# The first unit's bias features: spread over the rows by TensorE instead of by a DMA round trip, with the first sampling hats moved among the first tiles

## The chip, the cores and the metric

The kernel runs on one core of one Trainium2 chip. The metric is the device time of one execution in microseconds. Before the change it is 891.61 us, the median of three runs (891.41 to 891.81). All engines named here belong to that one core: TensorE (PE, with its weight loads PEld), VectorE (DVE), ScalarE (ACT), GpSimd (POOL) and SyncE (SP), which only issues DMAs.

## The reference

Two layers of the same block run over an image batch of 2 x 128 x 32 x 32. The part that matters is the attention with a learned position bias. Each of 8 groups (16 channels each) gets 64 keys, whose places come from a small convolution (offsets) and where the image is sampled bilinearly. Every one of the 1024 queries sees every key through a bias made by a small network on the signed logarithm of their distance:

```python
off = tanh(einsum('bchw,oc->bohw', gelu(conv(qg, off_dw_w) + off_dw_b), off_pw_w)) * OFF_SCALE
kv = grid_sample(xn, vgrid_scaled)                       # bilinear, 64 keys for each group
pos = grid_q[:, :, None, :] - grid_kv[:, None, :, :]     # 1024 queries x 64 keys x (x, y)
bias = sign(pos) * log1p(abs(pos))
bias = relu(bias @ cpb_w1 + cpb_b1)                      # 2 -> 32
bias = relu(bias @ cpb_w2 + cpb_b2)                      # 32 -> 32
bias = (bias @ cpb_w3 + cpb_b3)                          # 32 -> 1
attn = softmax(qh @ kh * scale + bias)
x = x + out_w @ (attn @ v) + out_b;  x = x + mlp(bn2(x))
```

## The kernel before

The work is cut into 4 segments (layer x image), each into 4 units (pairs of groups, 128 keys on 128 partitions after packing), each unit into 16 steps (2 halves of the queries x 8 strides of keys). So there are 256 steps. One step `g` is: DVE's `first_layer(g)` writes one buffer `h1` (128 x 2048) as the maximum of an x-term and a y-term; PE's `corrections` put a bf16 correction into two PSUM pairs; PE's `layer2(g)` multiplies `h1` by the second layer's weights in 16 tiles of 32 x 32; ACT's `relu2` empties the pairs; PE's `layer3` adds into the scores. There are three `h1` buffers, so DVE may be three steps ahead of PE.

The x- and y-terms (`hxy`) need, for each unit, the features of 128 keys laid over rows in another way than they were computed: key on the free axis, hidden unit on the partitions, each value repeated over 32 partitions. Before the change all 16 units get that layout by DMA: SP stores `feat` to DRAM (`store_features`), loads it back broadcast (`load_features`), and DVE's `hidden_terms` scales it in place.

Nothing is scheduled by a planner. Each engine runs a list of its own: first the list `PROLOGUE` in its order, then step by step its part of the step and behind it the stages that a table puts at that step (`LATE_SLOTS` for what the first segment still owes, `BEFORE_SLOTS` and `AFTER_SLOTS` for later segments). Engines meet only through semaphores. Eight banks of PSUM serve as three pairs handed out in the order in which PE fills them (`ring()`, `turn`, `filled`, `emptied`) and two score banks.

The first segment's own preparation stands in the prologue: normalised image, queries, convolution, offsets, positions, then two branches. One leads to the features and to the first `h1`. The other leads to the sampling weights: PE's `spread` lays the 64 x 2 key coordinates over all partitions, ACT's `spread_out` and eight `distances` take absolute distances, DVE's `hats` turn them into hat functions (`hat_x`, `hat_y`, the latter in `big`), DVE's `hat_products` multiply them into eight `bilinear` pieces, and PE's `sample` uses them. On DVE the prologue ends with `hats`, `hats`, `hidden_terms`. `hat_products` stand behind step 2, `sample` at step 3. PE's `keep_busy` runs four dummy matmuls at the start and four more once the terms are there.

On SP's queue the first segment is stored as features, one part of the `fy` weights (`fy_part`), the load of unit 0, the other `fy` parts, and then `load_fy`, which waits until all six `fy` stores are in DRAM.

Of the kernel before, what the change touches and what calls it, by code (L numbers as in the profile page):

```python
# [10 lines left out]
ALU = mybir.AluOpType  # L11
# [10 lines left out]
HID = 32  # L22
# [10 lines left out]
PAIRS = G // 2  # L33
# [32 lines left out]
for _name, _n in [("ident", 128), ("gridq", W), ("gridkv", 2), ("neg_x", 1), ("neg_y", CHUNKS), ("ones", 32), ("own", 2),  # L66
# [39 lines left out]
LATE_SLOTS = {("dve", "hat_products", 0): 2, ("dve", "hat_products", 1): 2,  # L106
              ("pe", "sample", 0): 3, ("dve", "sample_out", 0): 4, ("pe", "keys_values", 0): 5,
              ("act", "keys_values_out", 0): 5}
# [57 lines left out]
RELEASES = {"up_last": MLP_PARTS, "spread": 2, "keys_values": 5, "attend": 2, "mlp_up": 2}  # L166
RING_STAGES = ("u_rows", "q", "image_t", "offset", "spread", "sample", "keys_values", "scores_t", "attend",
# [35 lines left out]
def build(nc, x_in, consts, weights, x_out, features_dram, fy_dram, reciprocals_dram):  # L203
    with ExitStack() as ctx:
# [44 lines left out]
        h2 = [[sb(f"h2_{j}{k}", [128, ROWS // 2, HALF]) for k in range(H2_BUFS)] for j in range(2)]  # L249
        w1y_of_key = sb("w1y_of_key", [128, 128])  # L250
# [39 lines left out]
        terms_ready = sem("terms_ready")  # L290
        w1y_ready = sem("w1y_ready")
# [70 lines left out]
        def _(sp):  # L362
# [73 lines left out]
            for unit in range(UNITS):  # L436
# [20 lines left out]
        def _(pool):  # L457
# [8 lines left out]
            stages = {"widen_max": widen_max}  # L466
# [3 lines left out]
            for g in range(LAST_STEP + 1):  # L470
                for name, n in PLAN["pool"].get(g, []):
                    stages[name](n)

        @block.scalar
        def _(act):
# [48 lines left out]
            def features(seg):  # L524

                if seg:
# [10 lines left out]
            def spread_out(seg):  # L537
# [4 lines left out]
                emptied("spread", seg, act.activation(key_y, here[:, bank(1)], ACT.Copy))  # L542

# [36 lines left out]
            def gelu_last(part):  # L580
                for c in range(MLP_PARTS):
# [5 lines left out]
                      "offset_tanh": offset_tanh, "features": features, "spread_out": spread_out,  # L587
# [23 lines left out]
        def _(dve):  # L611
# [9 lines left out]
            def first_layer(g):  # L621
# [4 lines left out]
                if g % UNIT_STEPS == 0:  # L626
                    dve.wait_ge(terms_ready, 2 * (unit + 1))
# [125 lines left out]
            def hidden_terms(unit):  # L753
# [3 lines left out]
                dve.wait_ge(feat_loaded[p], 16 * ROWS * (unit // 2 + 1))  # L757
# [82 lines left out]
            for name, n in PLAN["dve"][-1]:  # L840
                stages[name](n)
# [347 lines left out]
```

## Time and profile before

| | |
|---|---|
| median of 3 runs | 891.61 us |
| the profiled execution, its own time | 894.96 us |
| its span, first to last instruction | 893.2 us |
| PE busy | 92% of the span |
| DVE busy | 81% |
| ACT busy | 74% |
| POOL busy | 7% |
| mean granted TensorE clock | 0.983 of full speed |

The profile is one execution. A busy share averages over the whole span, so a question on the start is put to the views of the start: the chain of waits (followed back from the last instruction, from each piece of work to what released it), the timeline (instructions in order of time, equal ones that follow each other merged, with the idle time before them) and the table of stretches (busy time of each engine in each stretch, with the granted TensorE clock). Step 0 of the 256 reaches PE at about 38 us, so everything before is a lead-in that no step overlaps.

### The profile page before, as it was taken

Reading aid. Unit: us, or ns where it says so; the run is one execution under the profiler, and the core shown is the slowest. Engines: PE = TensorE matmul, PEld = TensorE weight load, DVE = VectorE, ACT = ScalarE, POOL = GpSimd, SP = SyncE. Lnnn points to the kernel's source line nnn. Section 1 sums busy time; section 2 is a strip of 40 time slices with the busy share of each in tenths; the row PEclk is TensorE's granted clock in tenths of the full one; section 3 lists DMA queues with packets and bytes.
Section 4 is the critical chain, followed back from the end, with each engine's and each line's share of the span. In section 5 each row is a group of like instructions: output and inputs, shape, how many; then the busy total and the mean of one; then the engine's idle time right before and its main releaser. Section 6 shows DMA issues by size and latency. Waiting matters only on the chain.

```text
span 893.2 us, 27554 instructions
## 1 busy us (share of the span) xinstructions
PE 820.4 (92%) x12486; PEld 235.6 (26%) x12486; DVE 727.8 (81%) x532; ACT 662.1 (74%) x742; POOL 62.5 (7%) x39
## 2 busy tenths in 40 slices
PE   4699998889999999988999999988999999999997
PEld 2222222222222222222222222222222222222224
DVE  5899898898868689799885879979888668989843
ACT  2468778968777688896776877797777668888863
POOL 1000101000010100101010010100101001010110
PEclk8699999999999999999999999999999999999999
DMA  4502020020200102002020200102002020200000
GB/s 167 118 3 49 2 48 3 12 66 2 63 15 17 34 3 49 12 19 49 2 62 15 48 1 14 37 12 57 11 5 60 14 48 3 73 3 3 3 15 24
DMA packets 18264, 27.67 MB, mean 31 GB/s; under 512 B 10980, under 2 KB 11620, under 8 KB 18148
## 3 DMA queue, kind: packets, MB, share of 16 engines
q1 hardware_dynamic: 18148, 25.91, 11.7%
q8 instruction: 99, 1.62, 0.8%
q14 instruction: 17, 0.14, 0.1%
HBM read 23.05 MB, written 2.74 MB: 29 GB/s over the span
## 4 chain that ended last, share of the span: by engine, by line
PE 68%; ACT 14%; DVE 10%; issue 7%; DMA 1%; SPq 0%; ACTq 0%; POOLq 0%
PE pair L887 24%; PE scores L905 22%; ACT h L481 7%; PE pair L861 6%; DVE h L629 5%; PE pair L1040 3%; PE scores L916 3%; PE pair L995 2%; DVE big L742 2%; PE pair L1031 2%; PE pair L1013 2%; PE scores L1001 1%; ACT big L548 1%; ACT big L577 1%; ACT L577 1%
## 5 line engine op out<-in xcount | busy, mean ns | idle before, releaser
L629 DVE TENSOR_TENSOR h<-hxy 128x2048 f32<-128x2048 f32 x256 | 582.6, 2303 | 71.8 <-PE pair L887 67.8
L481 ACT ACTIVATE h<-pair 128x1024 f32<-128x1024 f32 x512 | 518.7, 1025 | 154.3 <-PE pair L861 113.5
L887 PE MATMUL pair<-h,wts 32*32 32x512 f32 x8192 | 300.0, 604 | 20.7 <-DVE h L629 7.7
L905 PE MATMUL scores<-h,wts 128*32 128x512 f32 x2048 | 275.6, 608 | 0.1
L463 POOL CAST neg_max_wide<-neg_max 128x512 fp32r<-128x512 f32 x32 | 59.3, 1853 | 808.0 <-DVE neg_max L765 808.0
L861 PE MATMUL pair<-fy,u_rows 32*128 32x512 bf16 x1024 | 102.6, 387 | 0.0
L887 PEld LDWEIGHTS pair<-h,wts 32*32 32x32 f32 x8192 | 66.0, 103 | 82.1 <-ACT h L481 36.2
L861 PEld LDWEIGHTS pair<-fy,u_rows 32*128 32x128 bf16 x1024 | 26.4, 91 | 217.2 <-issue 217.2
L905 PEld LDWEIGHTS scores<-h,wts 128*32 128x32 f32 x2048 | 42.0, 108 | 156.2 <-issue 147.5
L995 PE MATMUL pair<-const,probs 128*128 128x128 f32 x128 | 20.1, 280 | 21.6 <-ACT h L481 20.8
L491 ACT ACTIVATE probs<-scores,wts 128x512 f32<-128x512 f32 x32 | 22.0, 689 | 23.7 <-PE scores L905 23.5
L765 DVE TENSOR_REDUCE neg_max<-pair 128x8 f32<-128x512 f32 x32 | 22.1, 690 | 21.4 <-PE pair L995 21.2
L916 PE MATMUL scores<-qpad,keys_t 128*32 128x512 f32 x256 | 33.3, 592 | 0.0
L1031 PE MATMUL pair<-work,wts 128*128 128x512 f32 x56 | 27.3, 613 | 0.4
L1040 PE MATMUL pair<-big,wts 128*128 128x512 f32 x56 | 25.9, 605 | 1.1 <-ACT big L577 1.0
L995 PEld LDWEIGHTS pair<-const,probs 128*128 128x128 f32 x128 | 13.4, 140 | 49.8 <-issue 48.1
L794 DVE SCALAR_TENSOR_TENSOR x<-pair,wts,x 128x512 f32<-128x512 f32 x7 | 5.3, 751 | 25.9 <-PE pair L1040 25.9
L569 ACT ACTIVATE probs<-scores,wts 128x512 f32<-128x512 f32 x32 | 21.9, 685 | 4.8 <-PE scores L1001 4.6
L577 ACT ACTIVATE big<-pair,wts 128x512 f32<-128x512 f32 x28 | 17.7, 684 | 8.5 <-PE pair L1031 8.4
L1001 PEld LDWEIGHTS scores<-ident_r,neg_max_wide 128*128 128x128 f32 x128 | 17.2, 190 | 24.4 <-issue 23.0
L1001 PE MATMUL scores<-ident_r,neg_max_wide 128*128 128x128 f32 x128 | 23.0, 302 | 0.6 <-POOL neg_max_wide L463 0.6
L548 ACT ACTIVATE big<-work,const 128x512 f32<-128x512 f32 x32 | 21.0, 721 | 0.0
(106 smaller groups left out, 359.9 us busy)
## 6 DMA issues: line engine op xcount, KB each, us to landing
hxy<-features_dram SPq DMA_DIRECT2D x64, 256.0 KB, 4.8
wts<-weights_dram SPq DMA_DIRECT2D x2, 960.0 KB, 8.3
att_den<-reciprocals_dram SPq DMA_DIRECT2D x7, 256.0 KB
x<-x_dram SPq DMA_DIRECT2D x2, 512.0 KB, 5.7
fy<-fy_dram SPq DMA_DIRECT2D x16, 64.0 KB
fy_dram<-fy_part SPq DMA_DIRECT2D x24, 32.0 KB, 3.9
out_dram<-x SPq DMA_DIRECT2D x3, 256.0 KB, 5.4
features_dram<-pos_sign SPq DMA_DIRECT2D x4, 128.0 KB, 2.5
```

The source lines that it names most:

```text
L463: pool.tensor_copy(neg_max_wide[:], neg_max[phase % 2][:].unsqueeze(2).broadcast_to([128, CHUNKS, NKV]))\
L481: emptied("z", 2 * g + j, act.activation(h2[j][g % H2_BUFS][:].rearrange("p r n -> p (r n)"), pair_of("z", 2 * g + j)[:], ACT.Relu))
L577: emptied("mlp_up", n, act.activation(mlp_h[:, c, bank(half % 2)], pair_of("mlp_up", n)[:, bank(k)], ACT.Gelu, bias=w(half // 2 // B, "mlp ...
L629: dve.tensor_tensor(h1[g % H1_BUFS][:].rearrange("p c (y x) -> p c y x", x=W), hx[unit % 2][:, :, t].unsqueeze(2).broadcast_to([128, CT, H ...
L861: return pe.matmul(z_of(g, r), u_rows[unit // PAIRS // B][key_rows(r)], y.unsqueeze(2).broadcast_to([32, H // 2, W]), **flags)
L887: ins = pe.matmul(z_of(g, r)[32 * c:32 * (c + 1)], w(l, "w2")[key_rows(r), key_rows(r)], h1[g % H1_BUFS][key_rows(r), c], start=r >= 2, st ...
L905: ins = pe.matmul(scores[phase % 2][32 * r:32 * (r + 1)], w(l, "w3")[:, 32 * t:32 * (t + 1)], h2[rows[0] // 2][step % H2_BUFS][:, r % 2], ...
L916: ins = pe.matmul(scores[phase % 2][k], keys_t[seg % 2][:, u, k], qpad[seg % 2][:, 1 + H // 2 * h:1 + H // 2 * (h + 1), 1:W + 1], start=Fa ...
L995: ins = pe.transpose(pair_of("scores_t", phase)[:, s], probs[:, unit % PAIRS, bank(h)][:, s], cst("ident"))
L1001: ins = pe.matmul(scores[phase % 2][:, 128 * k:128 * (k + 1)], neg_max_wide[:, 2 * k:2 * (k + 1)].rearrange("p n j -> p (n j)"), ident_r[: ...
L1031: ins = pe.matmul(pair_of("mlp_up", n)[:, bank(k)], w(half // 2 // B, "mlp_w1")[:, 128 * c:128 * (c + 1)], xn2[:, bank(half % 2)], start=T ...
L1040: ins = pe.matmul(pair_of("mlp_down", half)[:, 0:HALF], w(half // 2 // B, "mlp_w2")[:, 128 * c:128 * (c + 1)], mlp_h[:, c, bank(half % 2)] ...
```

## The change

For unit 0 alone, the DRAM round trip of the features goes. PE's new `first_spread` writes the features straight into two PSUM pairs: 64 matmuls for each pair, each 32 rows by 32 columns with 64 moving columns, whose weight is one column of the identity repeated 32 times, so that it copies one key's features to 32 partitions. The four matmuls that follow each other use the four diagonal 32 x 32 tiles and write four different partition groups of the same PSUM columns. From the first pair ACT makes half of the terms (`first_terms`, two activations with scale and bias), from the second DVE makes the other half (two `tensor_scalar`). ACT needs the negated `w1y`, which DVE computes ahead of `norm1` (`neg_w1y`).

Orders move with it. On PE `u_rows` and four `keep_busy` matmuls stand before `offset`; `first_spread` stands behind `spread`; the second `keep_busy` now waits for DVE's `first_terms`. On DVE `hats` leave the prologue: the first stands behind step 1, the second behind step 2, and DVE's half of `hat_products` behind step 3. The other half of `hat_products` goes to POOL. `sample`, its copy and `keys_values` stand one step later. On SP all six `fy` stores come first, then the store of the features, `load_fy`, and the load of unit 1, which no longer waits for the terms of unit 0.

```diff
 PROLOGUE = {
-    "pe": ["q", "image_t", "offset", "spread", "u_rows"],
-    "act": ["q_out", "image_t_out", "conv_gelu", "offset_tanh", "features", "spread_out"] + ["distances"] * 4,
+    "pe": ["q", "image_t", "u_rows", "keep_busy", "offset", "spread", "first_spread", "first_spread"],
+    "act": ["q_out", "image_t_out", "conv_gelu", "offset_tanh", "features", "spread_out", "first_terms"] + ["distances"] * 4,
     "dve": ["norm1", "w1y_rows", "conv_products", "conv_products", "conv_sum", "conv_sum", "positions", "features_sign",
-            "fy_weights", "hats", "hats", "hidden_terms"],
+            "fy_weights", "first_terms"],
+    "pool": ["hat_products"],
 }
-LATE_SLOTS = {("dve", "hat_products", 0): 2, ("dve", "hat_products", 1): 2,
-              ("pe", "sample", 0): 3, ("dve", "sample_out", 0): 4, ("pe", "keys_values", 0): 5,
...
+LATE_SLOTS = {("dve", "hats", 0): 1, ("dve", "hats", 1): 2, ("dve", "hat_products", 1): 3,
+              ("pe", "sample", 0): 4, ("dve", "sample_out", 0): 5, ("pe", "keys_values", 0): 6,
...
-                if unit == 1:
-                    sp.wait_ge(terms_ready, 2)
...
-            for unit in range(UNITS):
+
+            store_fy(0, (0, 1, 2))
+            store_features(0)
+            load_fy(0)
+            for unit in range(1, UNITS):
...
+            def hat_products(n):
+
+                pool.wait_ge(hats_ready, 1)
+                for k in range(CHUNKS // 2):
+                    pool.tensor_tensor(bilinear[:, k], hat_y[:, k], hat_x[:], ALU.mult).then_inc(bilinear_ready[0], 1)
...
+            def first_terms(n):
+
+                act.wait_ge(first_scale_ready, 1)
+                wait_filled(act, "first_spread", 0)
+                here = pair_of("first_spread", 0)[:].rearrange("p (j a q) -> p a j q", a=2, q=W)
+                for xy, scale_of, bias_of in ((0, w(0, "w1x"), w(0, "b1")), (1, neg_w1y[:], 0.0)):
+                    out = hxy[0][:, xy].rearrange("p c t q -> p (c t) q")[:, 0:CT * STRIDES // 2]
+                    ins = act.activation(out, here[:, xy], ACT.Identity, bias=bias_of, scale=scale_of)
+                    emptied("first_spread", 0, ins)
...
-                if g % UNIT_STEPS == 0:
-                    dve.wait_ge(terms_ready, 2 * (unit + 1))
+                if g == 0:
+                    wait_emptied(dve, "first_spread", 0)
+                    wait_emptied(dve, "first_spread", 1)
+                elif g % UNIT_STEPS == 0:
+                    dve.wait_ge(terms_ready, 2 * unit)
...
+            def first_terms(n):
+
+                wait_filled(dve, "first_spread", 1)
+                here = pair_of("first_spread", 1)[:].rearrange("p (j a q) -> p a j q", a=2, q=W)
+                half = CT * STRIDES // 2
+                out = [hxy[0][:, xy].rearrange("p c t q -> p (c t) q")[:, half:2 * half] for xy in range(2)]
+                emptied("first_spread", 1, dve.tensor_scalar(out[0], here[:, 0], w(0, "w1x"), w(0, "b1"), ALU.mult, ALU.add))
+                emptied("first_spread", 1, dve.tensor_scalar(out[1], here[:, 1], w(0, "w1y"), -1.0, ALU.mult, ALU.mult))
...
+            dve.tensor_scalar(neg_w1y[:], w(0, "w1y"), -1.0, None, ALU.mult).then_inc(first_scale_ready, 1)
...
+            def first_spread(n):
+
+                pe.wait_ge(feat_ready, 1)
+                turn("first_spread", n)
+                half = CT * STRIDES // 2
+                for j in range(half):
+                    for r in range(ROWS):
+                        key = 32 * r + half * n + j
+                        ins = pe.matmul(pair_of("first_spread", n)[key_rows(r), 2 * W * j:2 * W * (j + 1)],
+                                        cst("ident")[key_rows(r), key:key + 1].broadcast_to([32, HID]),
+                                        feat[key_rows(r), 0:2 * PAIRS:PAIRS], start=True, stop=True)
+                filled("first_spread", n, ins)
...
-            pe.wait_ge(terms_ready, 1)
-            keep_busy(4)
+            wait_emptied(pe, "first_spread", 1)
+            keep_busy()
```

PE's order in the lead-in before the change, from the dummy matmuls to the first step (`scores<-keys_t` is `keep_busy`, `pair<-const,coord` is `spread`, `pair<-wts,w1y_of_key` is `u_rows`, `pair<-h_0,wts` is `layer2`):

```order
L1073 MATMUL scores<-keys_t 128x512 x4
L940 MATMUL pair<-work,wts 128x512 x2
L947 MATMUL pair<-const,work 128x128 x8
L955 MATMUL pair<-wts,conv_act 64x8 x2
L964 MATMUL pair<-const,coord 128x128 x8
L934 MATMUL pair<-wts,w1y_of_key 128x128
L1073 MATMUL scores<-keys_t 128x512 x4
L861 MATMUL pair<-fy,u_rows 128x512 x2
L887 MATMUL pair<-h_0,wts 32x512 x16
```

and after it (`pair<-pos_sign,const` is `first_spread`, since `feat` is the tile `pos_sign`):

```order
L1119 MATMUL scores<-keys_t 128x512 x4
L976 MATMUL pair<-work,wts 128x512 x2
L983 MATMUL pair<-const,work 128x128 x8
L970 MATMUL pair<-wts,w1y_of_key 128x128
L1119 MATMUL scores<-keys_t 128x512 x4
L991 MATMUL pair<-wts,conv_act 64x8 x2
L1000 MATMUL pair<-const,coord 128x128 x8
L1012 MATMUL pair<-pos_sign,const 32x64 x128
L1119 MATMUL scores<-keys_t 128x512 x4
L897 MATMUL pair<-fy,u_rows 128x512 x2
```

`u_rows` and one block of dummy matmuls moved ahead of `offset`, and 128 small matmuls stand between `spread` and the last dummy block.

DVE's order around the first steps before the change (`hat_x`, `big` 128x2048 are `hats`, `hxy` is `hidden_terms`, `h_...` one step's first layer, `big<-big,hat_x` the products, `sampled` the copy behind `sample`):

```order
L733 TENSOR_SCALAR hat_x<-hat_x 128x512
L736 TENSOR_SCALAR big<-big 128x2048 x2
L758 TENSOR_SCALAR hxy<-hxy,wts 128x1024
L759 TENSOR_SCALAR hxy<-hxy,wts 128x1024
L826 TENSOR_SCALAR scale<-wts 128x1 x2
L629 TENSOR_TENSOR h_0<-hxy 128x2048
L629 TENSOR_TENSOR h_1<-hxy 128x2048
L629 TENSOR_TENSOR h_2<-hxy 128x2048
L742 TENSOR_TENSOR big<-big,hat_x 128x512 x8
L629 TENSOR_TENSOR h_0<-hxy 128x2048
L629 TENSOR_TENSOR h_1<-hxy 128x2048
L749 TENSOR_TENSOR sampled<-pair,const 128x128
```

and after it:

```order
L793 TENSOR_SCALAR hxy<-pair,wts 128x512
L794 TENSOR_SCALAR hxy<-pair,wts 128x512
L861 TENSOR_SCALAR scale<-wts 128x1 x2
L655 TENSOR_TENSOR h_0<-hxy 128x2048
L655 TENSOR_TENSOR h_1<-hxy 128x2048
L759 TENSOR_SCALAR hat_x<-hat_x 128x512
L762 TENSOR_SCALAR big<-big 128x2048
L655 TENSOR_TENSOR h_2<-hxy 128x2048
L762 TENSOR_SCALAR big<-big 128x2048
L655 TENSOR_TENSOR h_0<-hxy 128x2048
L768 TENSOR_TENSOR big<-big,hat_x 128x512 x4
L655 TENSOR_TENSOR h_1<-hxy 128x2048
```

The hats now stand between the first layers of steps 1, 2 and 3, and four of the eight products are gone from DVE. They stand on POOL, whose list in the changed kernel runs so (the last two rows wait for the hats):

```order
L461 UNCONDITIONAL_BRANCH [waits barrier_Pool_Activation_PE_DVE_SP_gather]
L479 MEMSET qpad 128x1156 x2
L480 MEMSET fy 128x1024
L475 ISA
L475 TENSOR_TENSOR big<-big,hat_x 128x512 [waits hats_ready]
L475 TENSOR_TENSOR big<-big,hat_x 128x512 x3
```

The ISA row stands ahead of the first product and waits for nothing; POOL had no such row there before.

## Rows read from the trace of the kernel before

**Rows 1.** The page: busy time, share of the span, instructions of each engine

```profile
PE 820.4 (92%) x12486; PEld 235.6 (26%) x12486; DVE 727.8 (81%) x532; ACT 662.1 (74%) x742; POOL 62.5 (7%) x39
```

**Rows 2.** Chain of waits, 20 to 54 us: start, length, what

```profile
20.41 3.80 PE pair L964 x16
...
25.44 5.02 ACT big L548 x8
...
33.38 6.69 DVE h L629 x3
40.07 4.81 DVE big L742 x8
44.88 2.21 DVE h L629
...
48.39 1.89 PE pair L976 x64
...
51.46 1.10 PE pair L887 x32
...
53.88 1.10 PE pair L887 x24
```

**Rows 3.** Timeline, PE: start, length, instruction, idle time before it

```profile
10.06 1.04 PE L947 MATMUL pair<-const,work 128*128 128x128 f32 x8
...
23.99 0.63 PE L934 MATMUL pair<-wts,w1y_of_key 128*128 128x128 f32 x2
...
32.49 5.82 PE L1073 MATMUL scores<-keys_t 128*128 128x512 f32 x8 [7.86 <-DVE hxy L758]
...
38.24 0.39 PE L861 MATMUL pair<-fy,u_rows 32*128 32x512 bf16 x2
...
47.23 1.15 PE L887 MATMUL pair<-h,wts 32*32 32x512 f32 x32 [1.52 <-DVE h L629]
```

**Rows 4.** Stretches: busy (instructions) of each engine; then TensorE's granted clock

```profile
16.00:18.00 2.00, 0.39 (x4) 0.30 (x4) 0.96 (x1) 0.51 (x2) 0.00 (x0) 0.58 0.00 0
...
20.00:22.00 2.00, 1.59 (x7) 1.59 (x8) 1.78 (x8) 0.38 (x1) 0.00 (x0) 0.50 0.09 15
...
36.00:38.00 2.00, 2.00 (x5) 0.72 (x3) 2.00 (x2) 0.00 (x0) 0.00 (x0) 0.80 0.97 229
...
48.00:50.00 2.00, 2.00 (x80) 1.69 (x67) 1.29 (x1) 1.03 (x1) 0.00 (x0) 1.00 0.04 8
```

**Rows 5.** Timeline, DVE, from the weights of fy to the terms

```profile
24.66 0.35 DVE L713 SCALAR_TENSOR_TENSOR u_full<-wts,const,pair 128x128 f32<-128x128 f32 x1 [2.65 <-PE pair L934]
...
28.03 0.43 DVE L733 TENSOR_SCALAR hat_x<-hat_x 128x512 f32<-128x512 f32 x1 [0.55 <-ACT big L548]
28.49 1.23 DVE L736 TENSOR_SCALAR big<-big 128x2048 f32<-128x2048 f32 x1
...
32.35 0.74 DVE L759 TENSOR_SCALAR hxy<-hxy,wts 128x1024 f32<-128x1024 f32 x1
```

**Rows 6.** Timeline, DVE and POOL side by side, at three later places

```profile
172.35 1.13 POOL L463 CAST neg_max_wide<-neg_max 128x512 fp32r<-128x512 f32 x1 [26.84 <-DVE neg_max L765]
172.93 1.10 DVE L759 TENSOR_SCALAR hxy<-hxy,wts 128x1024 f32<-128x1024 f32 x1
...
193.31 4.48 DVE L629 TENSOR_TENSOR h<-hxy 128x2048 f32<-128x2048 f32 x2
...
198.68 4.90 DVE L629 TENSOR_TENSOR h<-hxy 128x2048 f32<-128x2048 f32 x2
198.83 2.61 POOL L463 CAST neg_max_wide<-neg_max 128x512 fp32r<-128x512 f32 x1 [25.35 <-DVE neg_max L765]
...
870.32 0.62 POOL L463 CAST neg_max_wide<-neg_max 128x512 fp32r<-128x512 f32 x1 [17.84 <-DVE neg_max L765]
```

**Rows 7.** Groups of instructions by shape: a DVE operation that reads PSUM

```profile
L794 DVE SCALAR_TENSOR_TENSOR x<-pair,wts,x 128x512 f32<-128x512 f32 x7 | 5.3, 751 | 25.9 <-PE pair L1040 25.9
```

**Rows 8.** Timeline, SP: the issue of the load of fy

```profile
30.65 2.81 SPq L416 DMA_DIRECT2D fy<-fy_dram x4
```

More of the change, by code:

```diff
@@ L161 @@
 LAST_STEP = max(max(at) for at in PLAN.values())
-RELEASES = {"up_last": MLP_PARTS, "spread": 2, "keys_values": 5, "attend": 2, "mlp_up": 2}
-RING_STAGES = ("u_rows", "q", "image_t", "offset", "spread", "sample", "keys_values", "scores_t", "attend",
+RELEASES = {"first_spread": 2, "up_last": MLP_PARTS, "spread": 2, "keys_values": 5, "attend": 2, "mlp_up": 2}
+RING_STAGES = ("u_rows", "first_spread", "q", "image_t", "offset", "spread", "sample", "keys_values", "scores_t", "attend",
                "project", "mlp_up", "mlp_down", "up_last")
@@ L249, in build @@
         h2 = [[sb(f"h2_{j}{k}", [128, ROWS // 2, HALF]) for k in range(H2_BUFS)] for j in range(2)]
+        neg_w1y = sb("neg_w1y", [128, 1])
         w1y_of_key = sb("w1y_of_key", [128, 128])
@@ L469, in _ @@
             pool.memset(fy[0][:], 1.0).then_inc(ones_set, 1)
-            for g in range(LAST_STEP + 1):
+            for g in range(-1, LAST_STEP + 1):
                 for name, n in PLAN["pool"].get(g, []):
@@ L524, in features @@
             def features(seg):
+                if seg == 1:
+                    wait_filled(act, "first_spread", 1)
                 if seg:
@@ L586, in _ @@
             stages = {"q_out": q_out, "gelu_last": gelu_last, "image_t_out": image_t_out, "conv_gelu": conv_gelu,
-                      "offset_tanh": offset_tanh, "features": features, "spread_out": spread_out,
+                      "offset_tanh": offset_tanh, "features": features, "first_terms": first_terms, "spread_out": spread_out,
                       "distances": distances, "attend_out": attend_out,
@@ L756, in hidden_terms @@
                 l, p = unit // PAIRS // B, unit % 2
-                dve.wait_ge(feat_loaded[p], 16 * ROWS * (unit // 2 + 1))
+                dve.wait_ge(feat_loaded[p], 16 * ROWS * (unit // 2 + p))
                 dve.tensor_scalar(hx[p], hx[p], w(l, "w1x"), w(l, "b1"), ALU.mult, ALU.add).then_inc(terms_ready, 1)
                 dve.tensor_scalar(hy[p], hy[p], w(l, "w1y"), -1.0, ALU.mult, ALU.mult).then_inc(terms_ready, 1)
+            def first_terms(n):
[5 more added lines that the diff above has]
+                emptied("first_spread", 1, dve.tensor_scalar(out[1], here[:, 1], w(0, "w1y"), -1.0, ALU.mult, ALU.mult))
             def score_max(phase):
@@ L830, in _ @@
                       "features_sign": features_sign, "hats": hats, "w1y_rows": w1y_rows, "conv_products": conv_products,
-                      "hat_products": hat_products, "sample_out": sample_out, "hidden_terms": hidden_terms,
+                      "hat_products": hat_products, "sample_out": sample_out, "hidden_terms": hidden_terms, "first_terms": first_terms,
                       "score_max": score_max, "divide": divide, "reciprocal": reciprocal,
@@ L1064, in down_last, with keep_busy @@
                 ins.then_inc(last_down, 1)
-            stages = {"project_last": project_last, "up_last": up_last, "down_last": down_last, "u_rows": u_of_layer, "q": q, "image_t": image_transpose, "offset": offset, "spread": spread,
+            def keep_busy(n=0):
+                for _ in range(4):
+                    pe.matmul(scores[1][:], keys_t[0][:, 0], keys_t[0][:].rearrange("p u k -> p (u k)"), start=True, stop=True)
+            stages = {"keep_busy": keep_busy, "first_spread": first_spread, "project_last": project_last, "up_last": up_last, "down_last": down_last, "u_rows": u_of_layer, "q": q, "image_t": image_transpose, "offset": offset, "spread": spread,
                       "sample": sample, "keys_values": keys_values, "scores_t": scores_transpose, "max_off": max_off,
                       "attend": attend, "project": project, "mlp_up": mlp_up, "mlp_down": mlp_down}
-            def keep_busy(n):
-                for _ in range(n):
-                    pe.matmul(scores[1][:], keys_t[0][:, 0], keys_t[0][:].rearrange("p u k -> p (u k)"), start=True, stop=True)
             pe.wait_ge(setup_done, 1)
-            keep_busy(4)
+            keep_busy()
             pe.wait_ge(const_loaded, 16)
```

7 lines of the change are left out of this document (4 added, 3 removed).

## The prediction

> **What bounds the kernel now.** I read the page's busy shares first [rows 1]: PE is at 92%, so in the steps the time is PE's, and 256 steps follow at PE's pace whatever the start does. The change touches only the lead-in and the first six steps, so its worth is one number: by how much PE's work at a fixed step, from which on PE waits no more for DVE, starts earlier or later. So I read the chain of waits from 20 to 54 us [rows 2]. It does not run through the DMA round trip that the change removes. It runs from PE's `spread` (20.41, 3.80 us) over ACT's distances (5.02 us) to DVE, and then stays on DVE: three first layers, eight products, one first layer. Only at 47.23 does it pass to PE. The timeline agrees: at 38.24 PE begins the first step straight behind its own dummy matmuls (32.49 plus 5.82), yet at 47.23 it has stood idle 1.52 us for DVE's fourth `h` [rows 3]. So until `sample` the limit is a chain of DVE instructions, not the moment at which PE may begin. From `sample` on PE runs without a gap of note: step 4's `layer2` at 51.46, step 5's at 53.88, 2.42 us apart [rows 2]. Step 5 is my fixed place.
>
> **The DVE chain, before and after.** Let T be the moment at which DVE has the last term of unit 0. Before, that is 32.35 + 0.74 = 33.09, and the first layers start 0.29 later, at 33.38 (two scale instructions stand between) [rows 2, 5]. Then 6.69 + 4.81 + 2.21 brings the fourth `h` to T + 14.0 = 47.09, and step 5's `layer2` follows 6.79 us behind it, of which 2.42 is step 4's own turn.
>
> After the change `sample` stands behind step 4, so the fifth `h` is the one that ends the chain, and only 6.79 - 2.42 = 4.37 us lie between its end and step 5's `layer2`. The chain in front of it: 0.29, five first layers at 6.69 / 3 = 2.23 = 11.15, the hats that move in (0.43 + 1.23 + 1.23, with hand-overs 2.9 [rows 5]), four products at 4.81 / 8 = 0.60 = 2.4. That is T + 16.74, without anything from POOL. Step 5 then starts at T + 21.11, against 53.88: with POOL free of charge the time moves by T - 32.77. So the hats are not gone, they are moved behind T, and the four products that leave DVE (2.4 us) do not quite pay for them (2.9 us).
>
> **What POOL's four products cost DVE.** Here the trace speaks against the change. POOL's cast of 128x512 takes 0.62 us alone. Beside DVE's first layer it takes 2.61 us, and DVE's two first layers there take 4.90 instead of 4.48 us; beside the scaling of the terms it takes 1.13 us, and the second scaling takes 1.10 instead of 0.74 us [rows 5, 6]. So POOL and DVE take turns, and each POOL instruction that gets in delays DVE's next one by 0.36 to 0.42 us, some 0.2 us less than its own length. The Trainium skill's page "SBUF — State Buffer", section "Who interferes with whom", says so too: a VectorE instruction with two SBUF inputs and a GpSimd instruction that reads SBUF exclude each other for a whole instruction; this trace agrees (4.90 against 4.48 us).
>
> No row has a two-input operation on POOL. It reads two operands where the cast reads one, so the bounds are one cast and two casts, 0.62 and 1.24 us, and the delay to DVE is 0.42 to 1.24 us. I take 1.0, near the upper end, since both inputs must be read. The four all stand between the first hat and the fifth `h`, where DVE has no idle time to give. That is 4.0 us on the chain (1.7 to 5.0). A gain is excluded, since POOL only adds turns. By the skill's "GPSIMD Engine Reference", section "3. Performance versus the Vector engine", a two-input operation of 2048 elements takes 4497 ns there, which makes an estimate of 1.1 us for 512; at that as the delay the shift would be 0.4 us longer, and no run here shows it yet. With 4.0 the time moves by **T - 28.77**.
>
> POOL's additional ISA row waits for nothing and can run from 3.7 us on, over 30 us before the hats; I cost it at nothing, and if it held the first product back by some us, the products would get in beside later first layers at the same price.
>
> **How early is T?** Up to the positions the chain is as before, plus one small DVE instruction (`neg_w1y`) ahead of `norm1`: 0.2 us, a little more than one of those two scale instructions. `u_rows` moves into PE's idle time and takes away DVE's wait of 2.65 us in front of `u_full` [rows 5]; DVE is then done with its weights at about 25, before it is needed. The dummy matmuls ahead of `offset` begin behind the transposes, which end at 11.1 [rows 3], and `u_rows`, so at about 11.6. They are 8 records of 512 columns; at the pace of `sample` below (26.5 ns for a quarter of 128 columns and four abreast, so 0.42 us for 512) that is 3.4 us. They end at 15, before `offset`, the four matmuls in the stretch from 16 to 18 [rows 4], and delay nothing.
>
> `spread`: 16 records in 3.80 us, at a clock of 0.50 (1.2 GHz) [rows 2, 4]. The stretch from 16 to 18 has 0.58 on average, so the clock fell at about 16.3, some 5 us behind the transposes' end [rows 3, 4]. Now the last dummy matmul ends 5.6 us ahead of `spread`, with only `offset` between. If the clock holds, `spread` takes half, 1.9 us; I take the low clock, since the one pause of that length that the trace shows lost it: PE is free at 23.99 + 0.2 = 24.2 [rows 3].
>
> `first_spread`: 128 fp32 matmuls are 256 records (two a matmul, as everywhere in this trace). The nearest row is `sample`, 64 records of 32-column tiles with four abreast and 128 moving columns, 1.70 us from start to start at clock 1.00, or 26.5 ns a record [rows 2, 4]. At that rate 256 records take 6.8 us, the upper end: it is what they cost if the issue sets the pace, and also if the columns do at half the clock. With 64 columns and the full clock it is half, 3.4 us, the lower end. The last dummy block of before started at the low clock at 32.49, and the clock was up within the stretch from 36 to 38 [rows 3, 4]; `spread` starts at 20.6, so most of `first_spread` should run at the full clock. I take 4.2 us.
>
> `first_terms` on DVE: two operations of 128x512 from PSUM. Half of the scaling from SBUF is 0.37, a heavier PSUM operation of that size is 0.75 [rows 5, 7]; I take 0.65 each, 1.3 in all, and 0.3 for the matmuls' end and the hand-over. T = 24.2 + 4.2 + 0.3 + 1.3 = **30.0**. ACT's half comes from the first pair, half of `first_spread` earlier, and is done before T; its eight distances (5.02 us) then end at about 33.5, before the first hat at T + 4.75.
>
> **What stays covered.** PE's dummy block now begins at T and takes 3.4 us (5.8 when it starts at the low clock [rows 3]); step 0 needs the `fy` load, which was issued from 30.65 for 2.81 us [rows 8] behind stores that now go first, so it lands about 2.5 us earlier. PE could start at about 33.5 to 36 instead of 38.24. That is worth nothing by itself: step 3 needs the fourth `h`, which DVE has at about T + 14. The cover of all this is some 8 us; beyond, PE's start would be the limit. The load of unit 1 goes earlier and is needed 16 steps later.
>
> **The sum.** T - 28.77 = 30.0 - 28.77 = **+1.2 us**. The profiled execution, 894.96 us with a span of 893.2, would become 896.2 and 894.4; it stands 3.35 us above the median of 891.61, which moves by the same amount, to **892.8**. Two earnings (the distances and the round trip out of the way, 3.1 us of T) are eaten by the hats behind T and by POOL's turns.
>
> **Rivals.** (1) *POOL costs DVE little.* For it: POOL's rows are rough, and the turns measured are only 0.42 us. At 1.7 us for the four the shift is 30.0 + 1.7 - 32.77 = -1.1 (890.5); at nothing -2.8 (888.8). Against: every cast beside DVE in rows 6 delays it.
>
> (2) *The clock holds from the dummy matmuls to `spread`.* Then PE is free at 22.7, held there by `u_full`, which must empty its pair, and T = 28.5: -0.3 (891.3); with (1) down to -2.6. For it: 5.6 us is hardly more than the 5 us after which it fell, and `offset` breaks the pause.
>
> (3) *The four diagonal tiles do not run abreast.* This one ends slower. A record of 64 columns alone takes 4 x 26.5 / 2 = 53 ns at the full clock. Two abreast give 6.8 us (T = 32.6, +3.8, 895.4), one at a time 13.6 us (T = 39.4, +10.6, 902.2). It decides from 4.8 us on, where the shift passes +1.8. Against it: `layer2` has 16 tiles in flight (32 records in 1.15 us, where one at a time would take some 13), but its row groups write different banks, while `first_spread`'s four write the same one, so no row shows this case. The skill's "TensorEngine Tiling (Array Packing)", section "Gotcha 1: PSUM Pressure", says that different row tiles cannot access the same PSUM bank at the same time; by that rule one at a time would hold.
>
> (4) *Nothing changes since PE's start is the limit.* Excluded by the 1.52 us that PE waits for DVE [rows 3].
>
> **Chances.** Forecast 0.38 (about 891.5 to 894.3), (1) 0.20, (2) 0.18, (3) 0.24. A measurement here can tell 0.2%, 1.8 us, from no change. Faster by more takes (1) near nothing, or (1) and (2) together: 0.21. Slower by more takes (3), or the forecast with POOL's upper price: 0.36. The rest, 0.43, is within 0.2%. The range runs from (1) with free products to (3) with two abreast and POOL's upper price: 888.6 to 896.8.
>
> **What would show it.** In the profile after: DVE's first terms end near 30 (T); the four products on POOL stand between 37 and 48 us and take 2 to 3 us each where they meet a first layer, and DVE's first layers and hats there are longer than 2.23 and 1.23 by about 1 us four times; PE waits 4 us or more for the fifth `h` ahead of `sample`; `first_spread` takes about 4.2 us for 256 records. The forecast is wrong if POOL's products leave DVE's durations alone, if `first_spread` takes over 6 us, or if PE waits for `fy` or for its dummy block rather than for DVE.

## The result, and the profile of the changed kernel

The change makes the kernel slower. Its median is 897.89 us (895.96 to 898.84), against 892.88 us for the kernel before. The ratio is 1.0048 (95% interval 1.0033 to 1.0063), about 4.3 us; the two medians lie 5.0 us apart. The forecast was 1.2 us, 892.8 us with a range to 896.8; the direction was right, the size was not. The profiled execution took 898.21 us with a span of 896.4 us, at a mean granted clock of 0.987.

The busy shares again tell little (compare [rows 1]): PE has its additional dummy and spreading matmuls, DVE has four products less and one small instruction more.

```profile
PE 828.2 (92%) x12750; PEld 242.1 (27%) x12750; DVE 730.0 (81%) x529; ACT 662.9 (74%) x744; POOL 72.8 (8%) x43
```

The chain of waits from 20 to 60 us (start, length, what) is the view that answers to [rows 2]:

```profile
20.12 3.78 PE pair L1000 x16
23.91 3.69 PE pair L1012 x170
27.59 0.42 issue
28.01 1.45 PE pair L1012 x86
...
29.48 0.81 DVE hxy L793
30.29 0.66 DVE hxy L794
...
31.23 4.50 DVE h L655 x2
...
45.02 4.56 DVE big L768 x4
49.59 2.21 DVE h L655
...
51.94 2.02 PE pair L923 x32
53.96 3.35 PE pair L1025 x64
...
58.49 1.10 PE pair L923 x32
```

It has the predicted shape: `spread` and `first_spread` on PE, the terms on DVE, then one long run of DVE instructions up to the fifth `h`, and PE from there. T, the end of the last term, is 30.95. The fifth `h` ends at 51.80, which is T + 20.85. Step 5's `layer2`, the fixed place of the prediction, starts at 58.49 against 53.88 [rows 2]: 4.61 us later. POOL's later casts, which follow the steps, stand 4.6 us later too until 142 us. There the profiled execution of before lost clock for two stretches and 1.3 us with it, and this one did not:

```profile
142.00:144.00 2.00, 2.00 (x23) 0.34 (x29) 2.00 (x3) 0.24 (x1) 1.10 (x1) 0.65 0.04 8
144.00:146.00 2.00, 2.00 (x35) 0.34 (x36) 1.03 (x1) 1.03 (x2) 1.51 (x1) 0.50 0.00 0
```

(Kernel before; columns as in [rows 4], the granted clock is the third number from the end.) So its two spans differ by 3.2 us and not by 4.6. Of the ten traces of this document two have this fall, the one of before and that of the hats in DVE's idle time, so it is put down to the execution and not to the change.

The stretches of the changed kernel show where its own clock fell:

```profile
18.00:20.00 2.00, 0.00 (x0) 0.00 (x0) 1.81 (x8) 1.55 (x3) 0.00 (x0) 0.85 0.00 0
20.00:22.00 2.00, 1.88 (x9) 1.88 (x10) 1.79 (x7) 0.09 (x1) 0.00 (x0) 0.50 0.07 16
...
46.00:48.00 2.00, 2.00 (x28) 0.27 (x12) 2.00 (x2) 1.02 (x1) 1.83 (x2) 0.67 0.03 8
...
52.00:54.00 2.00, 2.00 (x36) 0.34 (x40) 1.99 (x1) 0.01 (x1) 0.00 (x0) 0.50 0.00 0
```

Just ahead of `spread` it is at the low level (0.50, 1.2 GHz), as predicted. But it falls again within 46 to 48, and is low while PE does step 4's `layer2` and `sample`. The timeline of PE (start, length, instruction, idle time before it) shows what came before:

```profile
45.17 1.15 PE L923 MATMUL pair<-h,wts 32*32 32x512 f32 x32 [3.02 <-DVE h L655]
...
51.94 2.02 PE L923 MATMUL pair<-h,wts 32*32 32x512 f32 x32 [3.58 <-DVE h L655]
53.89 3.42 PE L1025 MATMUL pair<-big,image_t 128*32 128x128 f32 x64
```

PE stood idle 3.02 us for the fourth `h` and 3.58 us for the fifth; the clock fell between the two waits. In the kernel before there was one wait of 1.52 us [rows 3], and the clock held. At the low level `layer2` takes 2.02 us instead of 1.15, and `sample` 3.42 instead of 1.89 on the chain [rows 2].

POOL's products beside DVE, from the timeline of the two engines:

```profile
37.41 10.43 POOL L475 TENSOR_TENSOR big<-big,hat_x 128x512 f32<-128x512 f32 x4 [33.73 <-DVE big L762]
```

```profile
36.10 1.23 DVE L762 TENSOR_SCALAR big<-big 128x2048 f32<-128x2048 f32 x1
37.24 2.29 DVE L655 TENSOR_TENSOR h<-hxy 128x2048 f32<-128x2048 f32 x1
39.45 2.31 DVE L762 TENSOR_SCALAR big<-big 128x2048 f32<-128x2048 f32 x1
41.67 3.35 DVE L655 TENSOR_TENSOR h<-hxy 128x2048 f32<-128x2048 f32 x1
44.94 4.64 DVE L768 TENSOR_TENSOR big<-big,hat_x 128x512 f32<-128x512 f32 x4
```

The hat ahead of POOL's first product takes 1.23 us, the one in the middle 2.31; the first layer behind it 3.35 instead of 2.29; DVE's four products 4.64 instead of 2.4. Those are four delays of about 1.08 us, as many as POOL has instructions (the products share two of them).

### The profile page after: what moved, and what is told of

It reads as the page before. It is cut to its first block, busy times and chain, and to the rows that moved or that the text cites. A ratio compares the mean times of both kernels' runs of the same rounds, so it can differ in the third digit from the quotient of the medians.

```text
span 896.4 us, 28086 instructions
## 1 busy us (share of the span) xinstructions
PE 828.2 (92%) x12750; PEld 242.1 (27%) x12750; DVE 730.0 (81%) x529; ACT 662.9 (74%) x744; POOL 72.8 (8%) x43
## 4 chain that ended last, share of the span: by engine, by line
PE 68%; ACT 13%; DVE 11%; issue 7%; DMA 1%; SPq 0%; ACTq 0%; POOLq 0%
PE pair L923 23%; PE scores L941 22%; ACT h L492 7%; PE pair L897 6%; DVE h L655 5%; PE pair L1089 3%; PE scores L952 3%; PE pair L1044 2%; DVE big L768 2%; PE pair L1080 2%; PE pair L1062 2%; PE scores L1050 1%; ACT big L600 1%; ACT L600 1%; PE pair L976 1%
```

## Experiments

Before these runs the theory was a sum of three: POOL's turns, the clock that falls while PE waits for DVE, and a T that is 0.95 us later than forecast. The rivals were that POOL's products cost DVE nothing that matters, that the removed round trip would have paid if the rest had been left alone, and that `first_spread` is slow for another reason than the clock. Where the texts on record use letters, P is the theory of POOL's turns, K that of the clock during the waits, C that of the clock ahead of `spread`, D that the round trip was not the limit, and G that the hole within `first_spread` hangs on the count of instructions. Each kernel ran in five rounds against the kernel before, whose own medians lie between 892.24 and 893.90 us in these series; so the kernels are compared by their ratios. The intervals of the changed kernel and of those that take back one part of it overlap, so what each part costs is read from the traces. The place of step 5's `layer2` is a second measure, from one execution of each and without the scatter that later falls of the clock bring: 53.88 us in the kernel before, 58.49 in the changed one. It has a scatter of its own: `spread` starts between 19.57 and 20.65 us in the ten traces, and that difference is there already at PE's first real matmul (7.59 to 8.68 us), ahead of all that the change moves but `neg_w1y`, which takes 0.15 us. Counted from the start of `spread`, step 5's `layer2` comes after 33.47 us in the kernel before and 38.37 in the changed one, 4.90 us later.

### All eight products on DVE

```diff
-    "pool": ["hat_products"],
...
-LATE_SLOTS = {("dve", "hats", 0): 1, ("dve", "hats", 1): 2, ("dve", "hat_products", 1): 3,
+LATE_SLOTS = {("dve", "hats", 0): 1, ("dve", "hats", 1): 2, ("dve", "hat_products", 0): 3, ("dve", "hat_products", 1): 3,
```

> The changed kernel, but the four products that POOL had stand on DVE again, all eight behind step 3. Theory P (POOL's turns hold up DVE, and the long waits of PE let its clock fall): the second hat and the first layer behind it shrink by about 1.0 us each to 1.23 and 2.2, the products become 4.8 us for eight instead of 4.56 for four, so the fifth h ends about 1.8 us earlier, at some 50.0 us; if PE's clock holds, step 5's layer2 begins 4.4 us behind that (54.4 instead of 58.49), and the time falls by 1.8 to 4.1 us against the changed kernel. Rival N (POOL's products cost DVE nothing that matters, the loss is in the hats or the spread): the fifth h comes 2.4 us later and the time rises by that.

Measured: 896.34 us, 1.0035 (1.0023 to 1.0047). From the chain:

```profile
39.36 1.14 DVE big L761
40.50 2.20 DVE h L654
42.70 4.81 DVE big L767 x8
...
49.86 1.39 PE pair L922 x32
51.25 3.26 PE pair L1024 x64
...
55.70 1.10 PE pair L922 x32
```

The hat and the first layer are back at 1.14 and 2.20 us, and eight products on DVE take 4.81 us where four took 4.56 beside POOL. The fifth `h` ends at 49.72, T (30.79) + 18.93, against T + 20.85 beside POOL. So POOL's turns are confirmed: handing DVE's four products to POOL saved DVE 2.4 us and cost it 4.3. The clock fell all the same, after a wait of 2.44 us, and `sample` took 3.26 us. So step 5's `layer2` comes at 55.70 and not at the 54.4 that were expected if the clock held, and the ratio falls by 0.0013, about 1.2 us, where 1.8 at the least were expected. This alone does not bring the kernel back to the time before.

### PE kept at work during its waits

```diff
...
+                if g in (3, 4):
+                    keep_busy(times=3)
                 if g < ALL_STEPS:
```

> The changed kernel with three dummy matmuls on PE behind the corrections of steps 3 and 4 each, where PE stands idle for DVE (3.0 and 3.6 us). Nothing else moves. Theory K (2.3 us of the loss is PE at half its clock from about 46 to 57 us): layer2 of step 4 takes 1.15 instead of 2.02 us, sample 1.9 instead of 3.4, step 5's layer2 begins at about 56.2 instead of 58.49, and the time falls by about 2.3 us, with the fifth h where it was (51.8). Rival (sample is slow because its inputs or PSUM are shared with something else): durations stay at 2.0 and 3.4 at a granted clock of 1.00, and the time stays.

Measured: 895.62 us, 1.0027 (1.0016 to 1.0039). PE's timeline:

```profile
48.10 2.84 PE L1119 MATMUL scores<-keys_t 128*128 128x512 f32 x6
51.40 1.15 PE L923 MATMUL pair<-h,wts 32*32 32x512 f32 x32 [0.45 <-DVE h L655]
52.48 1.95 PE L1025 MATMUL pair<-big,image_t 128*32 128x128 f32 x64
...
55.55 1.17 PE L923 MATMUL pair<-h,wts 32*32 32x512 f32 x32
```

The dummy matmuls fill the waits, the clock stays at 1.00 in every stretch from 42 to 58, `layer2` takes 1.15 and `sample` 1.9 us. The chain has step 5's `layer2` at 55.62, 4.36 us behind the fifth `h` (51.26): the 4.37 of the prediction. DVE's chain is untouched (T + 20.86). The theory of the clock holds, and its price is the 2.3 us between 4.36 and the changed kernel's 6.69.

### The spread alone

The spread and `first_terms` stay; hats, products and `sample` go back to their places of before, on DVE and PE, and ACT makes its distances ahead of its half of the terms.

```diff
-    "act": ["q_out", "image_t_out", "conv_gelu", "offset_tanh", "features", "spread_out", "first_terms"] + ["distances"] * 4,
+    "act": ["q_out", "image_t_out", "conv_gelu", "offset_tanh", "features", "spread_out"] + ["distances"] * 4 + ["first_terms"],
...
-            "fy_weights", "first_terms"],
-    "pool": ["hat_products"],
+            "fy_weights", "hats", "hats", "first_terms"],
...
+LATE_SLOTS = {("dve", "hat_products", 0): 2, ("dve", "hat_products", 1): 2,
+              ("pe", "sample", 0): 3, ("dve", "sample_out", 0): 4, ("pe", "keys_values", 0): 5,
...
```

> The changed kernel's spread of the features, but the hats, products, sample and keys stand where they were before the change, POOL has no products, and ACT makes the eight distances ahead of its half of the terms. Theory D (before the change T, the end of the terms, was set by ACT's distances and the hats in front of the terms, not by the round trip): T is about 32.9 us against 33.09 before, step 5's layer2 at about 53.7, and the time is that of the kernel before within 1 us. Rival (the round trip through DRAM set T): T falls to about 31 and the time by about 2 us below the kernel before.

Measured: 892.94 us, 0.9993 (0.998 to 1.0005): no difference. The chain:

```profile
26.71 3.78 ACT big L570 x6
...
30.51 1.23 DVE big L761
...
32.45 0.66 DVE hxy L793
```

It goes past `first_spread` altogether, over ACT's distances and the hats as before, and the terms end at 33.11 (33.09 before). Step 5's `layer2` is at 53.90. So the round trip was not what the kernel waited for, and taking it away earns nothing where the hats stand ahead of the terms.

### The moved hats alone

The kernel before, with its DMA round trip; only the hats, products and `sample` move, all of it on DVE.

```diff
-            "fy_weights", "hats", "hats", "hidden_terms"],
+            "fy_weights", "hidden_terms"],
...
+LATE_SLOTS = {("dve", "hats", 0): 1, ("dve", "hats", 1): 2, ("dve", "hat_products", 0): 3, ("dve", "hat_products", 1): 3,
+              ("pe", "sample", 0): 4, ("dve", "sample_out", 0): 5, ("pe", "keys_values", 0): 6,
...
```

> The kernel before with its DMA round trip, but with the hats and all eight products among the first tiles as in the change (no POOL), sample and keys one step later. Theory D2 (the DMA had the features in place at about 29.8, two scalings take 1.5): T is about 31.4, hardly later than the 30.95 of the changed kernel; the fifth h ends at T + 19.1 = 50.5, step 5's layer2 at about 54.9, 1.0 us later than before, and the time is 0.5 to 2 us above the kernel before and within 0.7 us of the run with the products on DVE. Rival S (the spread itself wins some us over the DMA): T stays above 32.5 and the time is over 1.5 us above the run with the products on DVE.

Measured: 896.44 us, 1.0034 (1.0021 to 1.0047). Now the chain runs over the DMA:

```profile
24.44 5.48 DMA hxy<-features_dram
...
29.94 0.81 DVE hxy L758
30.75 0.66 DVE hxy L759
```

T is 31.42, and with the spread in its place (the first experiment) 30.79. But `spread` itself starts 0.52 us earlier there (19.78 against 20.30), and counted from it T comes after 11.12 and 11.01 us: the new path is worth some 0.1 us of T. The two kernels' times agree within their intervals. Moving the hats behind T, with `sample` a step later, is what slows this kernel: it puts 2.9 us of hats between T and the fifth `h`, PE waits 4.27 us for that `h`, and the clock falls (`layer2` 2.02 us, `sample` 3.16). The expectation left that fall out, as the prediction did: step 5's `layer2` comes at 56.86 and not at about 54.9, and the time is 0.34% above the kernel before, about 3 us, not 0.5 to 2.

### The clock held up to the spread

```diff
-    "pe": ["q", "image_t", "u_rows", "keep_busy", "offset", "spread", "first_spread", "first_spread"],
+    "pe": ["q", "image_t", "u_rows", "keep_busy_6", "offset", "keep_busy_2", "spread", "first_spread", "first_spread"],
...
```

(`keep_busy_6` and `keep_busy_2` are six and two dummy matmuls.)

> The changed kernel with PE's dummy matmuls ahead of the spread moved and added to: six instead of four ahead of offset and two behind it, so that PE has no pause of over about 1.5 us up to spread. Theory C (spread and the first two thirds of first_spread ran at half the clock, since it had fallen at about 19.7 us): spread takes 1.9 instead of 3.78 us, first_spread's first 170 records 2.6 instead of 3.7, T comes about 3 us earlier (28 instead of 30.95), and the time falls by about 3 us against the changed kernel, PE's clock at the fifth h being as it is there. Theory G, on the pause inside first_spread behind record 170 (0.42 to 1.76 us, no semaphore ended it): if it hangs on the count of instructions ahead of it, it comes some 8 records earlier here, behind record 162; if it hangs on a semaphore or on the second pair, it comes behind 128 or stays at 170. Rival (first_spread is paced by the issue of instructions): the records keep 21.7 ns each at the full clock and T gains only 1.9.

Measured: 896.12 us, 1.0031 (1.0019 to 1.0043). PE's timeline:

```profile
20.13 2.05 PE L1000 MATMUL pair<-const,coord 128*128 128x128 f32 x16 [0.71 <-DVE coord L706]
22.14 2.51 PE L1012 MATMUL pair<-pos_sign,const 32*32 32x64 f32 x162
25.97 1.53 PE L1012 MATMUL pair<-pos_sign,const 32*32 32x64 f32 x94 [1.33 <-issue]
```

`spread` takes 2.05 us and T comes at 29.03, 1.92 us earlier than in the changed kernel. All of it reaches step 5's `layer2` (56.55), and the second fall of the clock is still paid (`sample` 3.33 us). Some 3 us were expected. `spread` brought 1.73 of the 1.92; `first_spread` is shorter by only 0.2, though its first records ran at 15 ns as expected.

The three rows also show why `first_spread` is slow. Its 256 records run at 15 to 17 ns each, but 1.33 us stand still between them, and nothing in the profile releases the wait. In the five kernels with four dummy matmuls ahead of `offset` that run `first_spread`, this hole stands behind record 170; here, as in the two later kernels with the same dummies, behind record 162: eight more records run ahead of it, and it comes eight records earlier. It is 0.42 us long in the changed kernel and 1.76 us in the first experiment, where the first 170 records run faster (2.64 instead of 3.76 us):

```profile
23.45 2.64 PE L1011 MATMUL pair<-pos_sign,const 32*32 32x64 f32 x170
27.85 1.42 PE L1011 MATMUL pair<-pos_sign,const 32*32 32x64 f32 x86 [1.76 <-issue]
```

So faster records mostly lengthen the hole: the rest starts 4.40 us after the first record here and 4.17 in the changed kernel (3.9 to 4.4 in the five, 3.3 to 3.8 in the three). That the hole's place hangs on the count of PE's instructions and not on the data is shown; that it is the supply of instructions is the reading that fits, and was not tried by itself.

### The hats in DVE's idle time, no POOL

From these five the costs were: POOL's turns 4.3 us less the 2.4 us of products taken off DVE, the clock during the waits 2.3, the clock at the start 1.9, which the kernel before pays too. Of the 4.90 us, counted from `spread`, 1.92 are POOL's and 2.33 the clock's; the 0.65 that is left is by subtraction the price of the hats behind T, less the earlier T, and no kernel ran with that alone. This version puts the first hat where DVE waits for `first_spread`, has ACT make two of the four distance stages ahead of the terms for it, puts the second hat behind step 0, drops POOL, puts the products back behind step 2, so that `sample` can stay at step 3, and puts four dummy matmuls before step 3's `layer2`.

```diff
+    "act": ["q_out", "image_t_out", "conv_gelu", "offset_tanh", "features", "spread_out", "distances", "distances", "first_terms", "distances", "distances"],
...
-            "fy_weights", "first_terms"],
-    "pool": ["hat_products"],
+            "fy_weights", "hats", "first_terms"],
...
+LATE_SLOTS = {("dve", "hats", 1): 0, ("dve", "hat_products", 0): 2, ("dve", "hat_products", 1): 2,
+              ("pe", "sample", 0): 3, ("dve", "sample_out", 0): 4, ("pe", "keys_values", 0): 5,
...
+                if g == 3:
+                    keep_busy(times=4)
```

> The changed kernel without products on POOL, with the first hat in the time in which DVE waits for first_spread (ACT makes four of its distances ahead of its half of the terms), the second behind step 0, all eight products behind step 2 and sample at step 3 as before the change, and four dummy matmuls on PE in front of step 3's first layer. By the chain: T stays at about 31.0, then 0.29 + 4 x 2.23 + 1.23 + 4.8 = 15.2 us to the fourth h at about 46.2 against 47.09 in the kernel before, PE at the full clock, step 5's layer2 at about 53.0 against 53.88, and the time 0.5 to 1.5 us below the kernel before. Rival (T waits for ACT, whose half now comes behind two distances, or DVE's hat is late): T is over 32 and nothing is won.

Measured: 892.43 us, 0.9997 (0.9986 to 1.0008). T is 31.49, in an execution whose `spread` started 0.5 us later than in the changed kernel. The fourth `h` ends at 46.63, and step 5's `layer2` starts at 53.41, 0.47 us earlier than before and 0.71 counted from `spread`. The cost of the change is gone; the 0.5 to 1.5 us that were expected beyond that are not shown by the times.

### Both together, and one wait less

The last two kernels take over the dummy matmuls of the fifth experiment (six ahead of `offset`, two behind); the second of them also lets PE's last dummy block start without waiting for the terms.

```diff
+    "pe": ["q", "image_t", "u_rows", "keep_busy_6", "offset", "keep_busy_2", "spread", "first_spread", "first_spread"],
...
```

> The last run's kernel with the dummy matmuls of the run before it (six ahead of offset, two behind). If both theories hold, T is about 28.5 to 29 (the first hat ends at about 27.5 on DVE, first_spread at about 27 to 28), the fourth h at about 44, step 5's layer2 at about 51, and the time is 2 to 4 us below the kernel before. Rival (the hats or fy's load become the last to arrive): T below 29 but PE's step 0 waits for fy beyond 36, or the fourth h stays at 46; then it is no faster than the last run.

```diff
-            wait_emptied(pe, "first_spread", 1)
             keep_busy()
```

> The last run's kernel (hats in the idle time and the clock held) with one wait less: PE's last dummy block no longer waits for DVE's terms but follows first_spread at once. There the clock fell at about 30 us, while PE waited 1.91 us for the terms; the block took 5.4 us, step 0 began at 34.9, and step 3's first layer at 45.9, though DVE had its fourth h at 44.57. Theory K again (PE's pauses cost twice, by the clock and by what it then has to catch up): the block runs from about 27.6 to 31.0 at the full clock, step 0 begins when the first h is there, at about 32.2, step 3's layer2 at about 44.7, and the time falls by about 1.2 us against the last run, 1.5 to 3 us below the kernel before. Rival (fy's load or the first h is what step 0 waited for): step 0 stays beyond 34 and the time stays at that of the last run.

Measured: 891.51 us, 0.9986 (0.9973 to 0.9998), and 891.80 us, 0.9987 (0.9975 to 0.9999). T is 29.53 and 28.53. In the first, DVE's fourth `h` is no longer what PE waits for:

```profile
20.57 2.07 PE pair L999 x16
...
25.10 1.33 ACT big L570 x2
...
26.91 1.23 DVE big L761
28.14 0.72 DVE hxy L792
...
29.57 5.40 PE scores L1118 x8
...
42.37 3.63 PE scores L1118 x8
46.00 1.07 PE pair L922 x32
...
52.58 1.10 PE pair L922 x24
```

Up to T the chain no longer runs over `first_spread` but over ACT's distances and the first hat. Behind T it runs over the dummy matmuls: a block that starts while the clock is low takes 5.40 us, and the block before step 3 pushes that `layer2` to 46.00. Without the wait the first block is out of the way, but then step 0 waits 0.90 us for the load of `fy` and step 1 1.66 us for the second `h`, the clock falls there, and the gain goes (`layer2` 2.02 us). From the second kernel's chain:

```profile
19.57 2.06 PE pair L999 x16
...
34.59 2.02 PE pair L922 x32
...
52.23 1.10 PE pair L922 x24
```

Its earlier T and step 5 are the execution's and not the kernel's: `spread` starts 1.00 us earlier than in the first. Counted from there T comes after 8.96 us in both, and step 5's `layer2` after 32.01 us in the first and 32.66 in the second, 0.65 later. Neither brought the 2 to 4 and 1.5 to 3 us that were expected. Both are faster than before by 0.1%, about 1.2 us, with an interval that ends just below 1, and their times cannot be told from each other. A shorter block before step 3 was not tried.

## Why the prediction was wrong

| step of the prediction | forecast | measured |
|---|---|---|
| PE free of `spread` | 24.2 | 23.9 |
| `first_spread` and hand-over | 4.5 | 5.58 |
| DVE's two terms | 1.3 | 1.47 |
| T | 30.0 | 30.95 |
| DVE's chain from T to the fifth `h`, with POOL | 20.74 | 20.85 |
| fifth `h` to step 5's `layer2` | 4.37 | 6.69 |
| shift at step 5 | +1.2 | +4.61 (+4.90 from `spread`) |

**The step that failed** is "only 6.79 - 2.42 = 4.37 us lie between its end and step 5's `layer2`". The 4.37 came from rows in which PE ran at the full clock [rows 2, 4]. The prediction itself made PE's wait for the fifth `h` longer ("PE waits 4 us or more"), but went on to cost the work behind that wait (3.58 us in the end) at full clock, although it had just read the clock's fall before `spread` from a pause of PE. The 2.32 us missing there are about two thirds of the 3.4 us by which it missed, and the second experiment gives them back to within 0.01 us.

**The second step** is the size of `first_spread`: 4.2 us and 0.3 for the hand-over were forecast, 5.58 were measured. The records are near the lower bound (15 to 17 ns each at the full clock; half of the row's 26.5 is 13.3). What was missing is a hole between records that no row of before shows, or rather the 4 us or so before which the records behind it do not start. The low clock over the first 85 or so records is not the cost: in the first experiment they ran at the full clock, and the rest started no earlier. The total lies within the bounds of 3.4 and 6.8, so this was a mis-sized term; with 0.17 more for the terms, less 0.3 for a `spread` that ended earlier, it makes T 0.95 late. `spread` started 0.5 us ahead of the 20.6 of the prediction, by the scatter of the lead-in; counted from its start T is 1.4 us late.

**What held.** DVE's chain came out 0.11 us long over 20.74. That it is so close is in part luck: without POOL the chain is 0.21 us shorter than the 16.74 of the prediction, and POOL's turns cost 0.3 more. POOL's turns were forecast at 4.0 and cost 4.3 (the chain of the first experiment, 18.93, less the four products' 2.4, is 16.53 from T without POOL, against 20.85). The row behind that, a cast that delays DVE by 0.36 to 0.42 us [rows 6], gave the kind of cost; the size needed the allowance for a second input. The Trainium skill's "SBUF — State Buffer", section "Who interferes with whom", says that a VectorE instruction with two SBUF inputs and a GpSimd instruction that reads SBUF exclude each other for a whole instruction, and the trace agrees for the first layer and the products, with about 1.08 us each time; the hat, with one input, was delayed by as much. The hidden work stayed hidden: the dummy block ran from 31.01 for 3.70 us, step 0 began at 34.64 (33.5 to 36 forecast), and PE met DVE's wait only at step 3. The additional ISA row delayed nothing, since POOL's first product starts at 37.41, right behind the hat that it needs.

**The rivals.** (1), POOL nearly free, falls with the four delays. (2), the clock holding up to `spread`, did not happen (0.85 in the stretch from 18 to 20, 0.50 after); made to happen, it brought T 1.92 us forward, where the forecast said 1.5 (PE was free at 22.18 and not held to 22.7). (3), the four diagonal tiles one after the other, falls: one at a time 53 ns a record would stand there, and 15 to 17 do. The Trainium skill's "TensorEngine Tiling (Array Packing)", section "Gotcha 1: PSUM Pressure", would have them exclude each other on a common bank; these rows differ, and the measurement decides. (4) fell as excluded. No rival held the fall of the clock behind the longer wait, though the mechanism was in the text. The ends of the range do not follow from their parts: these give 888.8 and 896.4, not 888.6 and 896.8; the measured 897.89 lies outside either way.

**What stays open.** What keeps the records behind the hole in `first_spread` from starting; and how much of the 3.7 us by which T came forward in the last two kernels (12.68 to 8.96 us from `spread`) can be kept, since there PE's own dummy blocks, the load of `fy` and the clock are late next, and only 1.46 and 0.81 us arrive at step 5.

## What to carry to other kernels

Where a change lengthens a wait of TensorE, price the work behind that wait at both levels of the clock, not at the level in the trace of before, and where the wait can't go, see if idle work in it is cheaper. Work moved from VectorE to GpSimd can cost VectorE more than it saves: four products that take VectorE 0.6 us each cost it 1.08 us each when GpSimd did them beside it. Whether it pays where VectorE has idle time to give was not tried. Compare places in two traces from an event that both share, here the start of `spread`, and not from the start of the span. Removing a transfer earns nothing before the chain of waits runs over it, and a kernel with that part alone shows this at the price of one run.

## What the hardware showed that was not expected

TensorE stood still once for 0.42 to 1.76 us within 256 small, independent matmul records, at a place that moves with the number of records issued before and not with the data; it was 0.42 us where the records ahead of it took 3.76 us and 1.76 where they took 2.64. Four diagonal 32 x 32 tiles that write one bank ran abreast at 15 to 17 ns a record of 64 columns. And one fall of the clock, in the middle of the steps, stands in two of the ten traces and costs some 1.3 us there (before against changed), as much as what the last two kernels gained, so that the place of a fixed step, counted from `spread`, was the steadier measure.
